# Setup of a recurrent-attention plus binarized-FFN layer: clip logarithms on GpSimd, split sums, other orders, idle products

## The reference

```
r = sigmoid(x Wr), k = x Wk, v = x Wv          (256 x 256 each)
scale_t = exp(t * log(sigmoid(decay)))          t = 0..2047, per column
cum = cumsum over t of k*v / max(scale_t, 1e-10);  state = cum * scale_t
y = rmsnorm(r * state) * ln_w;   x1 = layernorm(x + y Wo)
w -> mean|w| (per output row) * sign(w)         for w1 (1024 x 256) and w2 (256 x 1024)
h = gelu(x1 bw1 + b1);   out = layernorm(x1 + h bw2 + b2)
```

## Time and profile before

| | |
|---|---|
| time, median of 3 runs | 821.13 us (821.13 to 821.78) |
| the profiled execution: time | 821.11 us |
| its span | 819.3 us |
| TensorE busy | 798.8 us, 97% |
| VectorE busy | 771.3 us, 94% |
| ScalarE busy | 679.9 us, 83% |
| GpSimd busy | 295.3 us, 36% |
| granted TensorE clock, mean | 0.998 |

### The profile page before, as it was taken

How to read it: one execution, slowest core, us unless ns; L and a number is a source line. 1 busy time by engine, 2 the same in 40 slices (tenths; PEclk the granted TensorE clock), 3 DMA queues, 4 the chain that set the end, 5 groups by cost and what they waited for, 6 DMA issues and landing times.

```text
span 819.3 us, 16575 instructions
## 1 busy us (share of the span) xinstructions
PE 798.8 (97%) x5174; PEld 505.7 (62%) x5174; DVE 771.3 (94%) x1472; ACT 679.9 (83%) x973; POOL 295.3 (36%) x572
## 2 busy tenths in 40 slices
PE   6989999999999999999999999999999999999986
PEld 4555666656666656666656666655666665666654
DVE  7998999999999999999999999999999999999887
ACT  7987888888888888888888888888888888887775
POOL 3343323344223344333344333344333334332344
PEclk9999999999999999999999999999999999999999
DMA  8513553434553434553434454444454344444313
GB/s 261 99 27 78 129 125 84 110 94 102 128 128 86 115 81 105 125 128 92 113 79 109 118 128 100 105 89 106 112 128 105 100 97 104 106 102 104 78 26 104
DMA packets 168286, 86.27 MB, mean 105 GB/s; under 512 B 128572, under 2 KB 163912, under 8 KB 168264
## 3 DMA queue, kind: packets, MB, share of 16 engines
q1 hardware_dynamic: 147288, 52.97, 27.5%
q0 software_dynamic: 4608, 16.78, 10.4%
q10 hardware_dynamic: 16368, 16.25, 5.6%
HBM read 20.45 MB, written 16.78 MB: 45 GB/s over the span
## 4 chain that ended last, share of the span: by engine, by line
PE 88%; DVE 4%; POOL 2%; ACT 2%; issue 2%; DMA 0%; SPq 0%; POOLq 0%; DVEq 0%; ACTq 0%
PE ps_r L375 28%; PE ps_o L496 26%; PE ps_f L446 19%; PE ps_r L446 6%; PE ps_o L401 6%; PE ps_o L406 3%; DVE hid_lo L1008 1%; DVE u L959 1%; ACT hid L678 1%; DVE u_st L967 0%; PE ps_s L383 0%; DMA x_in<-in_L_attn_x_dram 0%; POOL root L1322 0%; POOL y_sqs L1310 0%; DVE state L923 0%
## 5 line engine op out<-in xcount | busy, mean ns | idle before, releaser
L496 PE MATMUL ps_o<-w2T,hid_hi 128*128 128x256 f16 x992 | 218.9, 273 | 3.4 <-DVE hid_lo L1008 3.0
L496 PE MATMUL ps_o<-w2T,hid_lo 128*128 128x256 f16 x992 | 218.8, 272 | 0.0
L375 PE MATMUL ps_r<-x_t,proj_hi 128*128 128x512 f16 x768 | 197.1, 379 | 1.2 <-issue 0.7
L446 PE MATMUL ps_f<-x_t,w1T 128*128 128x512 f16 x768 | 181.7, 379 | 1.6 <-DVE x_t L992 1.3
L678 ACT ACTIVATE hid<-ps_f,rows_c,f_scale 128x512 f32<-128x512 f32 x192 | 145.2, 774 | 42.2 <-PE ps_f L446 37.1
L1008 DVE SCALAR_TENSOR_TENSOR hid_lo<-hid,hid_scale,hid_hi 128x1024 f16<-128x1024 f32 (+1 forms) x136 | 160.3, 1222 | 0.9 <-POOL hid_hi L1343 0.6
L1310 POOL TENSOR_TENSOR y_sqs<-y_sq 128x512 f32<-128x512 f32 x32 | 46.7, 1459 | 309.6 <-ACT y_sq L653 309.6
L375 PEld LDWEIGHTS ps_r<-x_t,proj_hi 128*128 128x128 f16 x768 | 74.7, 98 | 91.3 <-issue 2.8
L713 ACT ACTIVATE hid_hi<-hid,hid_scale 128x2048 f16<-128x2048 f32 (+2 forms) x72 | 127.9, 1778 | 3.2
L446 PEld LDWEIGHTS ps_f<-x_t,w1T 128*128 128x128 f16 x768 | 74.9, 98 | 79.7 <-issue 1.6
L375 PE MATMUL ps_r<-x_t,proj_lo 128*128 128x512 f16 x384 | 114.2, 379 | 0.2 <-DVE proj_lo L1084 0.2
(11 more groups left out here) (191 smaller groups left out, 1332.2 us busy)
## 6 DMA issues: line engine op xcount, KB each, us to landing
x_in<-in_L_attn_x_dram SPq DMA_DIRECT2D x32, 512.0 KB, 4.1
res<-b_row POOLq DMA_DIRECT2D x32, 512.0 KB, 4.5
out_dram<-res ACTq DMA_DIRECT2D x31, 512.0 KB, 2.9
w_in<-in_L_ffn_w_dram SPq DMA_DIRECT2D x2, 1024.0 KB, 8.8
x_t<-x_st SPq DMA_TRANSPOSE x59, 3.7
b_row<-in_L_ffn_b_dram SPq DMA_DIRECT2D x1, 512.0 KB, 12.7
proj_in<-in_L_attn_Wk_dram SPq DMA_DIRECT2D x1, 256.0 KB, 3.8
proj_in<-in_L_attn_Wv_dram SPq DMA_DIRECT2D x1, 256.0 KB, 4.1
```

Source lines behind the costliest of these rows:

```text
L375: last = nc.tensor.matmul(ps_r[:, m, :], w[:, m, dc, ec * P:(ec + 1) * P], xx[:, :, dc, :], start=(n == 0), stop=(n == 3 * DC - 1))
L446: last = nc.tensor.matmul(f1_bank[hc % NF], w1T[:, hc, dc, :], xx[:, :, dc, :], start=(dc == 0 and n == 0), stop=(dc == DC - 1 and n == 1))
L496: last = nc.tensor.matmul(o_tok[:, tt, :], hh[:, hc, tt * P:(tt + 1) * P], w2T[:, :, hc, :], start=(hc == 0 and n == 0), stop=(hc == HC - ...
```

## The change

Five things, all in the setup:

- The clip exponents of pieces 1, 2 and 3 are written by GpSimd (`clip_logs_pool`, 128x512 float32, two for each piece), in the form that VectorE used. VectorE's `clip_logs(1)` and ScalarE's `clip_excess` and the constants for it are gone; `clip_table` has one form for all pieces. GpSimd does piece 1 ahead of its first `unscales`, piece 2 and half of 3 behind the second, the other half behind the third.
- VectorE: `wo_maxima` stands ahead of the low part of the third projection; the x bound between k_sb and kvg of chunk 0. In the first chunk behind F1 the order is scan of chunk 2 (without its gate product), `yl`, `block_sums`; the gate product comes behind the last `hl`, and `x1l_rows` one `hl` earlier. The factor of w2 (`alpha2`) is scaled by GpSimd in `diagonal`.
- ScalarE: `clip_table(1)` stands behind the first tanh; the signs of w2 stand two places earlier; w2's two absolute sums are apart, the first ahead of `yh(1)`, the second ahead of the fourth gelu; `yh(1)` stands ahead of all gelus.
- GpSimd: `y_scale(1)` ahead of `ysqs(1)`; `diagonal` behind `root_rms(1)` and `unscales(3, 3)`.
- TensorE: five idle products ahead of the transposition of the rows, ten behind it, ahead of x. In `O(1, 1)` the row sums stand behind the second low part instead of ahead of O.

```diff
@@ TensorE
-                if k < 2:
+                if k == 0:
                     sum_rows(c)
...
                 low(1).then_inc(s_o, 1)
+                if k == 1:
+                    sum_rows(c)
                 low(2)
...
                 pe.wait_ge(s_ident, 1)
+                idle_products(ps_f[:, 1, :], 5)
                 pe.wait_ge(s_rows_in, 48)
                 nc.tensor.transpose(ps_rows, rows[:, :], ident[0:n, 0:n]).then_inc(s_rows_t, 1)
+                idle_products(ps_f[:, 1, :], 10)
                 pe.wait_ge(s_x_in[0], 16)
@@ ScalarE
-                if n < 2:
-                    act.wait_ge(s_clip, DC * n + DC)
+                if n == 0:
+                    act.wait_ge(s_clip, DC)
                 else:
-                    act.wait_ge(s_excess, DC * n - DC)
+                    act.wait_ge(s_clip_pool, DC * n)
...
                 proj_split_hi(1)
-                clip_table(1)
                 proj_split_hi(2)
                 xsq(1, 0, 1)
-                clip_excess(2)
                 r_gates(0, 0, (0,))
-                clip_table(2)
+                clip_table(1)
                 xh(1, 1, slot=1)
                 signs(w1_in, w1_sgn, s_w1_in, s_sgn)
-                xsq(2, 0, 2)
+                ysq(0, (0,))
                 r_gates(0, 0, (1,))
                 wo_split_hi()
-                ysq(0, (0,))
+                xsq(2, 0, 2)
                 ysq(0, (1,))
                 r_gates(1, 1, (0,))
-                clip_excess(3)
+                clip_table(2)
                 yh(0)
                 xh(2, 2, slot=2)
+                signs(w2_in, w2_sgn, s_w2_in, s_sgn2)
                 clip_table(3)
                 nc.scalar.activation(warm[:, :], ones_col[:, :], ACT.Gelu)
                 r_gates(1, 1, (1,))
-                signs(w2_in, w2_sgn, s_w2_in, s_sgn2)
...
-                act.wait_ge(s_sgn2, 1)
-                alphas2()
                 x1h(0, 1)
                 ysq(1, (1,), y=y_second)
                 r_gates(2, 2, (1,))
+                alphas2((0,))
+                yh(1, y_second)
                 act.wait_ge(s_ready, 1)
-                gelu(0, range(0, 1))
-                yh(1, y_second)
-                gelu(0, range(1, 2))
+                gelu(0, range(0, 2))
                 act.wait_ge(s_ready, 2)
                 hh(0, pairs[0])
-                gelu(0, range(2, 4))
+                gelu(0, range(2, 3))
+                alphas2((1,))
+                gelu(0, range(3, 4))
@@ VectorE
             proj_maximum(2)
-            clip_logs(1)
             proj_split_lo(1)
...
-            proj_split_lo(2)
+            wo_maxima()
+            proj_split_lo(2)
...
-                kvs(0, 0, 0)
-                take_xbound(1, 1)
-                wo_maxima()
+                kvs(0, 0, 0, between=lambda: take_xbound(1, 1))
...
-                scans(2, 2, 0)
+                scan_state(2, 2, 0)
+                yl(1, y_second)
                 block_sums(1)
-                yl(1, y_second)
                 mean_sq(1)
...
                 hl(0, pairs[1], first=True)
+                x1l_rows(1, 1)
                 hl(0, pairs[2], first=True)
-                x1l_rows(1, 1)
                 hl(0, pairs[3], first=True)
+                scan_gate(2, 2, 0)
                 scans(2, 2, 1)
@@ GpSimd
-            nc.gpsimd.tensor_scalar(neg_log[:, :], dec_c[:, 1, :], -1.0, 1.0, ALU.mult, ALU.mult).then_inc(s_nlog, 1)
+            def clip_logs_pool(n, dcs=range(DC)):
+                pool.wait_ge(s_setup_a, 2)
+                part = slice(n * CH, (n + 1) * CH)
+                for dc in dcs:
+                    nc.gpsimd.tensor_scalar(clip_g[:, dc, part], steps[:, part], dec_c[:, 1, dc:dc + 1], -LOG_CLIP,
+                                            ALU.mult, ALU.min).then_inc(s_clip_pool, 1)
+            clip_logs_pool(1)
             pool.wait_ge(s_winv, 1)
             unscales(0, 0)
...
                 scales(1, 1)
                 unscales(1, 1)
+                clip_logs_pool(2)
+                clip_logs_pool(3, (0,))
                 ysqs(0)
...
                 unscales(2, 2)
+                clip_logs_pool(3, (1,))
                 root_rms(0)
                 root_u(0)
+                y_scale(1)
                 ysqs(1)
-                y_scale(1)
                 y_unscale(1)
                 scales(3, 3)
-                diagonal()
                 root_rms(1)
                 unscales(3, 3)
+                diagonal()
```

42 lines of the change are left out of this document (18 added, 24 removed).

## The result

The kernel after takes 825.38 us (median of 6 runs, 824.22 to 827.24), the kernel before 821.15 (6 runs, 821.10 to 821.78): ratio 1.0051, 95% interval 1.0038 to 1.0064. It is half a per cent slower, clear of the noise. The forecast was 820.4 with a range to 821.4. The outcome is rival C's: TensorE's granted clock fell, though not behind the two waits that C named. The profiled execution took 824.97 us for a span of 823.2, 3.86 more than before's 821.11.

What follows compares the result with a forecast made beforehand. TensorE bounds the loop, so the gain is how far its gapless start at 63.14 moves: 1.65 - 0.15 - 0.6 - 0.2 = 0.7 us, 821.1 to 820.4 us, range 819.1 to 821.4.

Steps and rivals of the forecast that it cites:

- rival C: TensorE's clock falls at F2's first pairs, waits of some 1.6 and 1.5 us: 823 to 825; chance 0.05.
- 1) to 3): Early setup on VectorE: third low part at 13.95, first scan 16.25, chunk 1's x low part 18.36, 1.65 us sooner.
- 4): Setup from 26.3 to 44: order of the chain as before, carrying the 1.65 us gain; work moved beside it is hidden.
- 7b: GpSimd's piece 2 logarithms, 0.69 us each, run ahead of the first gate product and delay it by 0 to 0.3.
- 7c: The last piece's second logarithm on GpSimd stands ahead of y_lo(0) at 28.9: 0 to 0.15 us.
- rival B: All collisions in full, 820.7, or 821.1 with the idle products' overrun; included logarithms over 2 us each; chance 0.2.
- 5): Idle products ahead of x speed TensorE early but nobody waits: 0, between a loss of 0.4 and a gain of 0.3.
- 6): Behind F1's first three tiles: mean square 0.37 later, residual u 0.15 later in old time, leaving 1.5 us without collisions.
- 7): VectorE and GpSimd collisions at three new places, from nothing to 1.05 us; 0.6 and 0.2 taken.
- a): y_sqs(1) on GpSimd gets in first, y_lo waits and comes 0.85 later, u 0.75 later: price 0.6 us.
- hold several waits and are at 1.00 throughout: Argument against the clock falling: stretches 40:60 and 60:80 of the profile before show granted clock 1.00 despite waits.
- nothing in the change touches it: The loop is bound by TensorE and unchanged, so the gain is how far TensorE's start at 63.14 moves.

Runs made afterwards that it cites:

- e16: Kernel after with y_sqs ahead of y_scale, block sums ahead of y_lo and TensorE's row sums ahead of O, as before the change: 824.21 us.
- e17: e16 without the fifteen idle products: 823.58 us.
- e2: Kernel after with two unused tiles for the dropped ones and everything behind F1's first tiles as before, so only early parts remain: 822.59 us.
- e7: e2 without the fifteen idle products: 823.94 us.
- e5: Kernel before with the fifteen idle products and nothing else: 0.9 us more in the median.
- e14: Kernel after with y_sqs ahead of y_scale on GpSimd and block sums ahead of y_lo on VectorE again: 825.14 us.
- e11: Kernel after with x1's low part behind the third hidden pair again; median not given, F2's second pair still waits 3.12 us.
- e3: Kernel before with only the change's late parts, the new orders behind F1's first tiles on all engines; median not given.
- e6: Kernel before with the wait for r moved between scan and gate product: 821.25 us, interval 0.9992 to 1.0011.
- e8: e2 with the wait for r ahead of the scan as before; median not given.
- e18: e17 with one small memset more on GpSimd in the setup: 821.80 us.

## Why the prediction was wrong, by its own steps

1) to 3) Right within 0.15 us: 13.90, 16.36 and 18.46 for 13.95, 16.25 and 18.36. The sum of bounds came at 25.07, not 24.65, F1 0.78 sooner, not 1.65.

4) The carried 1.65 was 0.78 by F1. The minimum's 2.0 us per logarithm for 0.69 is the mis-sized term of 7b and 7c: 0.2 taken, and 0.87 gone by F1. The rows show where 0.63 of it went: 0.23 at the gate product at 23.34 and 0.40 at y_lo at 29.86, both beside a logarithm (7c had put 0 to 0.15 on the second). For the other 0.24 no run shows the cause. Its row was another form of the instruction, a product and a sum. I had written 2 us each only as a footnote to rival B.

5) "0, between a loss of 0.4 and a gain of 0.3": in the kernel before they cost 0.9 in the median, in other pairs between a loss of 0.6 and a gain of 1.4 (e16 and e17, e2 and e7). x was not delayed (its transposes start at 5.4 in e5). The idea that they can only delay by overrunning x did not include what comes with a faster TensorE: it then waits for Wv, and with 1.36 us of that or more its clock falls again at 10.

6) **The step that failed.** It forecast u 0.15 later in old time and so 1.5 ahead; u came 0.8 behind. It priced the move of the row sums by its 0.37 us and did not compare the new time of the mean square with the start of hid_lo. What counted was the order at 50.2: the mean square at 50.2 meets hid_lo, and the root is kept out for its whole length (1.99 for 1.02). I had seen that "rms also had to wait out the hid_lo beside it" in the kernel before, and took that for the same wait again; there only rms met it (0.43 us), the root had gone ahead. e14 against e16 shows it: with the row sums back ahead of O the root is free (1.02 for 2.00).

7) a) happened as written (y_sqs 1.96, y_lo 1.80), but e14 shows that it decided nothing: u is 0.17 sooner without it, by the shift of the root. b) and c) are the mis-sized term of 4).

C) Right in its size (823 to 825 for 825.4) and wrong in its place and its chance, 0.05. It named the spreading of the first pairs, two waits of 1.6 and 1.5. e11 shows that x1's low part is not the cause; e3, e11 and e16, whose next wait is only 0.44 to 0.89, show that one wait of 2.0 us or more is enough. That 40:60 and 60:80 "hold several waits and are at 1.00 throughout" was no evidence against it, since the longest of them behind 40 was 1.29. The step from which it follows is 6, which moved TensorE and u but never took the one from the other: the second pair is later by u's 0.80 and GpSimd's pause of 0.35 (1.16), and the first pair is done 1.16 sooner (57.65 for 58.81), so that the wait of 0.80 becomes 3.12.

That "nothing in the change touches it", the loop, was wrong as a reading of the change, since the wait for r moved in every chunk, though e6 shows that this costs nothing. It was wrong as a forecast by 1.16 at chunk 5 in the kernel after, and by 1.2 behind chunk 30 in e2, e7 and e8, where a margin of 0.08 us decided which engine was first.

## What to carry to other kernels

Where work is moved so that one engine runs ahead, look for the wait that grows in front of it and add up its whole length. Here 1.65 us of waiting ahead of F2's second pair left the clock up, and 2.00 brought it down and cost 2.4 us by chunk 2 (e18 and e17). These are two executions at one place and not a limit to plan by: at 10 us a wait of 1.36 was followed by the lower clock too. Before pricing a collision, find which two instructions start within 0.3 us of each other on VectorE and GpSimd, in the whole kernel, and ask which will be first. This kernel lost 1.3 us to four memsets on an idle GpSimd, so a change to GpSimd's program needs a control with the same number of instructions.
